# A chain of four blocks: the norm of a block's first batch moved into the tail of the block ahead, and value projections moved to another burst and bank

## The reference, cut to what matters

```python
x = x + tanh(g_xattn[0]) * cross_attention_A(layernorm(x), ctx, mask, bias)   # 16 heads of 16, 512 keys
x = x + tanh(g_ffn[0])   * gated_mixture_B(layernorm(x))                      # 8 heads of 64, causal
x = x + tanh(g_xattn[1]) * cross_attention_C(layernorm(x), ctx)               # 16 heads of 64, 512 keys
x = x + tanh(g_ffn[1])   * product_key_experts_D(layernorm(x))                # top-8 of 64*64 experts
```

```python
q = xn @ w_q; k, v = split(ctx @ w_kv)             # per batch: 512 x 1024 each
attn = softmax(q / 8 @ k.T)                        # per head: 512 x 512
out = (attn @ v) @ w_out + b_out                   # times tanh(gate)
```

## Time and profile before

| | |
|---|---|
| median of three runs | 2357.6 us (2354.5 to 2362.8) |
| the profiled execution: its own time, its span | 2359.9 us, 2358.1 us |
| granted clock of TensorE, mean | 0.974 |
| TensorE busy | 2194.5 us (93%) |
| VectorE busy | 1688.5 us (72%) |
| ScalarE busy | 866.5 us (37%) |
| GpSimd busy | 118.2 us (5%) |
| block A | 0 to 376 us of the span |
| block B | 376 to 1090 us |
| block C | 1090 to 1694 us |
| block D | 1694 to 2358 us |

### The profile page before, as it was taken

The page is one execution under the profiler, slowest core; times in us unless marked ns, Lnnn a source line. Parts: engine busy times, 40 slices in busy tenths (PEclk is TensorE's granted clock), DMA queues, the critical chain, the costliest instruction groups (busy, mean ns, idle before and its releaser), DMA issues. The chain is left out here.

```text
span 2358.1 us, 45622 instructions
## 1 busy us (share of the span) xinstructions
PE 2194.5 (93%) x18214; PEld 1476.8 (63%) x18244; DVE 1688.5 (72%) x4536; ACT 866.5 (37%) x2003; POOL 118.2 (5%) x128
## 2 busy tenths in 40 slices
PE   7999986979999999998899999999779999999998
PEld 3555543444664755775445545555568898989897
DVE  6788873757557556544777777767578888989895
ACT  5787871150330321311555555545321112121110
POOL 3542201000000000000000000000000000000000
PEclk9899987999999999999999999999999999999999
DMA  5011103000000002001000000000200000000000
GB/s 169 22 40 42 27 9 147 0 1 0 1 1 1 1 1 107 1 1 47 1 1 1 1 1 1 1 1 1 107 37 1 2 2 11 2 10 2 1 11 10
DMA packets 23730, 48.62 MB, mean 21 GB/s; under 512 B 4960, under 2 KB 13408, under 8 KB 22880
## 3 DMA queue, kind: packets, MB, share of 16 engines
q1 hardware_dynamic: 23520, 45.71, 5.7%
HBM read 37.57 MB, written 2.10 MB: 17 GB/s over the span
## 5 line engine op out<-in xcount | busy, mean ns | idle before, releaser
L2022 PE MATMUL banks<-work,big 128*128 128x128 f32 x2048 | 251.4, 277 | 0.2 <-issue 0.2
L2022 PEld LDWEIGHTS banks<-work,big 128*128 128x128 f32 x2048 | 245.2, 192 | 4.7 <-issue 0.3
L928 PE MATMUL banks<-big,work 128*128 128x256 f32 x1024 | 241.2, 379 | 3.6 <-issue 3.3
L2133 ACT ACTIVATE work<-banks 128x512 f32<-128x512 f32 x128 | 76.5, 598 | 411.4 <-PE banks L2022 406.7
L854 PE MATMUL banks<-big,work 128*128 128x512 f32 x512 | 221.2, 593 | 0.0
L539 ACT ACTIVATE work<-banks,work 128x512 f32<-128x512 f32 x256 | 174.1, 686 | 121.9 <-DVE work L628 121.8
L928 PEld LDWEIGHTS banks<-big,work 128*128 128x128 f32 x1024 | 195.0, 190 | 33.9 <-issue 1.9
L1689 ACT ACTIVATE work<-work 128x512 f32<-128x512 f32 x256 | 181.0, 711 | 0.0
L854 PEld LDWEIGHTS banks<-big,work 128*128 128x128 f32 x512 | 96.8, 190 | 119.8 <-issue 119.6
L628 DVE TENSOR_REDUCE work<-banks 128x2 f32<-128x1024 f32 x128 | 150.5, 1217 | 14.9 <-PE banks L430 14.9
L1132 DVE CUSTOM_DVE_ANT_0 work<-banks,work 128x512 f32<-128x512 f32 (+3 forms) x128 | 57.7, 488 | 133.2 <-PE banks L870 132.7
(11 more groups left out here) (219 smaller groups left out, 3826.9 us busy)
## 6 DMA issues: line engine op xcount, KB each, us to landing
big<-in_bias SPq DMA_DIRECT2D x16, 256.0 KB, 4.6
big<-in_B_val SPq DMA_DIRECT2D x8, 512.0 KB, 6.9
big<-in_B_out SPq DMA_DIRECT2D x1, 4096.0 KB, 18.7
big<-in_D_downT SPq DMA_DIRECT2D x1, 4096.0 KB, 12.8
big<-in_D_up SPq DMA_DIRECT2D x1, 4096.0 KB, 22.1
work<-work SPq DMA_DIRECT2D x120, 32.0 KB, 2.0
big<-big SPq DMA_DIRECT2D x64, 32.0 KB, 2.0
wc<-in_ctxT SPq DMA_DIRECT2D x1, 2048.0 KB, 7.9
```

The source lines that it names most:

```text
L928: last = eng.matmul(XO[qt // 2][:, qt % 2 * D:(qt % 2 + 1) * D], spread[:, c % NG, qt * P:(qt + 1) * P], w_out[:, c, :], start=False, stop ...
L2022: last = eng.matmul(HP[n % 2][:, q * P:(q + 1) * P], down[:, kc * ELO + n * NJ + q, :], xnT[par][:, kc, :], start=(kc == 0), stop=(kc == K ...
```

## The change

Three edits in one. The norm of batch 0 of B is done in the last steps of A (one part at the end of each of the steps LAST - 3 to LAST + 2), and the norm of batch 0 of C in the steps 4 to 11 of B's last batch; for this `Norm` objects and their semaphores are made before the blocks, in a region of their own, and `xstage` lies at the same place in all three blocks. In B the wait for the constants moves from the head of each engine's stream to the first use: VectorE ahead of `pick_experts(0)`, ScalarE in `take_hits`, TensorE in `choose` (`CONSTS` is 5 + A.groups as before). In C a value projection is issued at u = 0, behind the keys of the next pair, into FB[1], and ScalarE takes it after the two exponentials of tile n; the first four, of batch 0, are issued in the first two bursts instead of before them. The waits on banks follow.

```diff
@@ -139,6 +139,13 @@
         m["s"] = s
+
+        m["stats"] = sb("stats", [P, 128])
+        small, stage = carve(m, "stats"), carve(m)(QT, D)
+        for name, heads, second in (("B", B_, None), ("C", C_, EPS)):
+            turned = Signal(nc, ctx, name + "_xn_transposed", KC)
+            m[name + ".turned"] = turned
+            m[name + ".norm"] = Norm(nc, ctx, m, name, small, second, QT, stage, (turned, KC))
         a_attention(nc, a, m)
@@ -335,7 +342,7 @@
         bo_loaded = ctx.enter_context(nc.semaphore("C_bo_loaded"))
-        xt_made, xt_ready = sig("xn_transposed", KC), sig("xnT_ready", KC)
+        xt_made, xt_ready = m["C.turned"], sig("xnT_ready", KC)
         k_made, k_ready, q_made, q_ready = sig("k_made", T), sig("k_ready", T), sig("q_made", T), sig("q_ready", T)
@@ -344,7 +351,7 @@
         out_made, y_ready, turn_done = sig("out_made", QT), sig("y_ready", QT), sig("x_updated", QT)
-        norm = Norm(nc, ctx, m, "C", take, EPS, QT, xstage, (xt_made, KC))
+        norm = m["C.norm"]
         NORM = [(1, 0), (1, 1), (2, 0), (2, 1), (3, 0), (3, 1), (4, 0), (4, 1)]
@@ -383,9 +390,9 @@
                     elif b == 0 and t == 1:
+                        eng.wait_ge(k_ready.sem, k_ready.at(0, 1))
+                    elif b == 0 and t == 2:
                         eng.wait_ge(v_ready.sem, v_ready.at(0, QT))
-                    elif b == 0 and t == 2:
-                        eng.wait_ge(k_ready.sem, k_ready.at(0, 2))
                     else:
@@ -397,13 +404,19 @@
                     if b == 0 and t == 1:
-                        eng.wait_ge(v_ready.sem, v_ready.at(0, QT))
-                    elif b or t:
+                        eng.wait_ge(v_ready.sem, v_ready.at(0, 1))
+                    elif t == 0 and b:
+                        eng.wait_ge(v_ready.sem, v_ready.at(b, QT - 1))
+                    elif t == 1:
+                        eng.wait_ge(v_ready.sem, v_ready.at(b, QT))
+                    elif 2 <= t <= 5:
+                        eng.wait_ge(v_ready.sem, v_ready.at(b, QT + t - 1))
+                    elif t >= 6 and b < B - 1:
+                        eng.wait_ge(v_ready.sem, v_ready.at(b + 1, t - 5))
+                    elif t >= 6:
                         eng.wait_ge(q_ready.sem, q_ready.at(b, t))
-                        if b > 0 and 3 <= t <= 6:
-                            eng.wait_ge(y_ready.sem, y_ready.at(b - 1, t - 2))
-                        if b < B - 1 and t == T - 1:
-                            eng.wait_ge(xt_ready.sem, xt_ready.at(b + 1, 1))
+                        if t == 6:
+                            eng.wait_ge(y_ready.sem, y_ready.at(b - 1, QT))
                     for kc in range(KC):
@@ -473,32 +486,39 @@
                 queries(0, 0)
-                for kt in range(QT):
-                    if kt >= 2:
-                        eng.wait_ge(v_ready.sem, v_ready.at(0, kt - 1))
-                    elif kt == 0:
-                        eng.wait_ge(k_ready.sem, k_ready.at(0, 1))
-                    else:
-                        eng.wait_ge(q_ready.sem, q_ready.at(0, 1))
-                    values(0, 0, kt, FB[kt % 2])
                 for b, t, u, n in bursts():
+                    if n == 2:
+                        eng.wait_ge(k_ready.sem, k_ready.at(0, 2))
+                        values(0, 0, 1, FB[0])
+                        eng.wait_ge(q_ready.sem, q_ready.at(0, 2))
+                        values(0, 0, 2, FB[1])
                     if n >= 2:
...
                         scores(b, t, u, n, i)
+                    if n == 0:
+                        values(0, 0, 0, FB[1])
+                    if n == 2:
+                        eng.wait_ge(v_ready.sem, v_ready.at(0, 2))
+                        values(0, 0, 3, FB[0])
                     after = (b, t + 1) if t < T - 1 else (b + 1, 0)
...
                         keys(*after)
+                    if u == 0 and n > 2:
+                        if b and 2 <= t <= 5:
+                            eng.wait_ge(y_ready.sem, y_ready.at(b - 1, t - 1))
+                        if b < B - 1 and t >= 6:
+                            eng.wait_ge(xt_ready.sem, xt_ready.at(b + 1, t - 5))
+                        if t == 0:
+                            values(b, 0, QT - 1, FB[1])
+                        elif t <= 4:
+                            values(b, 1, t - 1, FB[1])
+                        elif b < B - 1:
+                            values(b + 1, 0, t - 5, FB[1])
                     if u == 1:
...
                             eng.wait_ge(k_ready.sem, k_ready.at(*after) + 1)
-                        if 1 <= t <= 4:
-                            values(b, 1, t - 1, FB[0])
-                        elif t >= 5 and b < B - 1:
-                            values(b + 1, 0, t - 5, FB[0])
-                        elif t == 0 and b > 0:
-                            values(b, 0, QT - 1, FB[0])
                         if b > 0 and 1 <= t <= 4:
@@ -509,9 +529,7 @@
                     if u == 1 and (b or t):
-                        if b < B - 1 or t <= 4:
-                            eng.wait_ge(v_ready.sem, v_ready.at(b, t + QT))
-                        elif t == T - 1:
+                        if b == B - 1 and t == T - 1:
                             eng.wait_ge(on_ready.sem, on_ready.at(b, T - 2))
@@ -566,25 +584,28 @@
-                norm.all_parts(eng, 0, norm.on_scalar)
-                for kt in range(QT):
-                    take_values(0, 0, kt, FB[kt % 2])
-
                 for b, t, u, n in bursts():
...
                         norm.on_scalar(eng, b + 1, NORM.index((t, u)))
+                    if n == 2:
+                        take_values(0, 0, 1, FB[0])
+                        take_values(0, 0, 2, FB[1])
                     if n >= 2:
...
                     spread_probs(n, 1)
+                    if n == 0:
+                        take_values(0, 0, 0, FB[1])
+                    if n == 2:
+                        take_values(0, 0, 3, FB[0])
+                    if u == 0 and n > 2:
+                        if t == 0:
+                            take_values(b, 0, QT - 1, FB[1])
+                        elif t <= 4:
+                            take_values(b, 1, t - 1, FB[1])
+                        elif b < B - 1:
+                            take_values(b + 1, 0, t - 5, FB[1])
                     spread_probs(n + 1, 0)
-                    if u == 1:
-                        if 1 <= t <= 4:
-                            take_values(b, 1, t - 1, FB[0])
-                        elif t >= 5 and b < B - 1:
-                            take_values(b + 1, 0, t - 5, FB[0])
-                        elif t == 0 and b > 0:
-                            take_values(b, 0, QT - 1, FB[0])
                     if n >= 2:
@@ -658,7 +679,6 @@
                 eng.wait_ge(s["x_loaded"], 16)
-                norm.all_parts(eng, 0, norm.on_vector)
                 for c in range(KC):
@@ -713,9 +733,9 @@
     vtok = wide(QT, A.width)
+    xstage, xnT = take(QT, D), take(KC, S)
     onT = [wide(T, S), take(T, S)]
     pickers = spare(GE, P // 2).bitcast(BF16)
-    xstage, xnT = take(QT, D), take(KC, S)
     qT, kT = take(2, S), spare(2, S)
@@ -734,7 +754,7 @@
         consts = ctx.enter_context(nc.semaphore("B_consts_made"))
-        xt_made, xt_ready = sig("xn_transposed", KC), sig("xnT_ready", KC)
+        xt_made, xt_ready = m["B.turned"], sig("xnT_ready", KC)
         gate_made, gate_ready, pick = sig("gate_made", 1), sig("gate_ready", 1), sig("pick_step", 6)
@@ -745,7 +765,8 @@
         turn_done = sig("x_updated", QT)
-        norm = Norm(nc, ctx, m, "B", take, None, QT, xstage, (xt_made, KC))
+        norm, following = m["B.norm"], m["C.norm"]
+        CONSTS = 5 + A.groups
@@ -911,6 +932,8 @@
                         eng.wait_ge(hit_ready.sem, hit_ready.at(b, 1))
+                        if b == 0:
+                            eng.wait_ge(consts, CONSTS)
                     if b or c:
@@ -930,7 +953,6 @@
                 eng.wait_ge(s["wb_loaded"], 48)
-                eng.wait_ge(consts, 5 + A.groups)
                 for c in range(KC):
@@ -1010,6 +1032,8 @@
                     eng.wait_ge(hit_turned.sem, hit_turned.at(b, 1))
+                    if b < 2:
+                        eng.wait_ge(consts, CONSTS)
                     if b >= 2:
@@ -1052,6 +1074,8 @@
                             norm.on_scalar(eng, b + 1, t * QT + i - 2)
+                        if b == B - 1 and 0 <= t * QT + i - 4 < following.parts:
+                            following.on_scalar(eng, 0, t * QT + i - 4)
                         if len(done) >= 2:
@@ -1183,6 +1206,10 @@
                             norm.on_vector(eng, b + 1, t * QT + i - 2)
+                        if b == B - 1 and 0 <= t * QT + i - 4 < following.parts:
+                            if t * QT + i == 4:
+                                eng.wait_ge(turn_done.sem, turn_done.at(0, QT))
```

(13 more changed lines are left out.)

## The result

The changed kernel takes **2323.7 us** (median of four runs, 2319.7 to 2327.0) where the kernel before takes 2359.0 in the runs beside it (2354.5 to 2362.8): a ratio of 0.985, 95% interval 0.9825 to 0.9875. Forecast was 2320, range 2312 to 2333. The profiled execution has a span of 2323.6 us and a time of its own of 2325.4; mean granted clock 0.977 for 0.974, TensorE busy 2191.2 us, VectorE 1687.2, ScalarE 868.8. The work is the same; of the 34.5 us by which the span is shorter, 31.2 are TensorE's idle time and 3.3 its busy time, which the clock makes longer or shorter.

What follows compares the result with a forecast made beforehand. TensorE's own work bounds the second stage's last batches; its waits at seams and in the third stage can be won. Gains 11.2 + 2.3 + 7.0 + 7.0 + 10.8 = 38.3 us off 2357.6 gave 2319.3, stated 2320, range 2312 to 2333.

Steps and rivals of the forecast that it cites:

- First seam: First to second stage: TensorE starts at 377.2 for 388.48, tail 1.2 us later included; 11.2 us gained.
- The clock term: Second stage's first chain, to the value projections: shorter if the clock stays high; 2.3 us gained, bounds 0 and 4.8.
- Second seam: Second to third stage: TensorE starts at 1090.3 for 1097.28, last batch no longer; 7.0 us gained.
- Start of C: Third stage's start: first scores 15.4 us earlier, less 7.0 for values and 1.4 more; net 7.0 us gained.
- The walk: Third stage, first scores to end of first weighing: 34.7 us, 1.4 more than before; bounds 31.3 and 38.
- The pairs: Third stage's head pairs, values moved to the first burst: 10.8 us gained in sum, bounds 0 and 20.
- Plain pairs: Third stage, six pairs with values but no output projection: 15.77 us, 0.92 less each, 5.5 in all.
- Pairs in which x is turned: Third stage, six pairs turning x in the second burst: 0.1 us less each, 0.6 in all.
- Pairs with a projection: Third stage, pairs with output projection: values' copy already covered; only small waits ahead of transposes won, 1.8 us with ends.
- The weighing's wait: Rival, third stage's pairs: ScalarE's queue brings the wait back, the 10.8 us are gone; 2334 us, chance 0.16.
- Clock held at the seams: Rival, seams and third stage's batch 0: clock stays high, 2.5, 1.7 and 2 us more gained; 2314, chance 0.17.
- The slower case: Rival, 28 pairs: ScalarE's wait for values delays exponentials, some 2 us of lateness per copy; at more 2376, chance 0.03.

Runs made afterwards that it cites:

- e4: Changed kernel with the waits for GpSimd's constants back at the head of the second stage on TensorE and ScalarE: 2331.4 us, ratio 0.9892.
- e5: Changed kernel with ScalarE's norm parts in the first stage's tail one step later, square root behind the last copy: 2320.4 us, ratio 0.9835.
- e2: Kernel before with only the norm of the third stage's batch 0 moved into the second stage's last batch: 2351.1 us, ratio 0.9961.
- e3: Kernel before with only the third stage's value projections moved to the first burst: 2341.7 us, ratio 0.9929.
- e1: Kernel before with only the first seam's edit, norm done ahead and constants awaited at first use: 2347.0 us, ratio 0.9953.
- e8: Changed kernel plus three unused ScalarE copies behind the copy of the values in each of 28 pairs: 2344.6 us, ratio 0.9946.
- e10: Changed kernel run again, unedited: 2319.6 us, ratio 0.9829.
- e9: e5 plus four unused matmuls on TensorE ahead of the first stage's last output projection: 2314.9 us, ratio 0.9813.
- e11: e9 plus four unused 128-column matmuls behind each short step of the second stage's first chain: 2314.2 us, ratio 0.9800.
- e6: Changed kernel with values still in the first burst but in their old bank, FB[0]: 2321.2 us, ratio 0.9839.
- e7: Changed kernel plus one unused ScalarE copy behind the copy of the values in each of 28 pairs: 2325.0 us, ratio 0.9863.
- e12: e9 run again, unedited: 2313.4 us, ratio 0.9805.

## Why the prediction was right

**First seam, 11.2 gained: right.** The idle time fell by 12.4 and the tail's wait rose by 2.40 - 1.21 = 1.2. e4 shows that the two edits share the gain evenly, e5 that the 1.2 are the table load's place. The weights and constants were covered as reckoned: the first value projection starts without a wait, and VectorE waits 6.58 us for constants and then 7.20 for TensorE. What had no term was A's own clock: A ended 6 us later than before in one profile and 1.5 in the next, of which 1.2 are the tail's. The medians' distances from 2320, 3.7 and -0.4, are no larger than that scatter.

**The clock term, 2.3 gained: too large.** With the 13.4 us of idleness ahead the chain took 14.1, 15.8 and 15.8 us (before, e2, e3), mean 15.2; with 1.0 us ahead and no fillers 13.4 to 15.1 in seven profiles (after, e1, e5 to e8, e10), mean 14.2. That is 1.0 where 2.3 stood. The middle of two bounds was a guess, and it weighed three causes: the idle stretch ahead, the wait for the moves before it, and the short waits in between. The first two are not what decides: e9 takes most of the wait for the moves away and the chain stays at 14.9. The third is: e11 fills the small waits inside the chain and it falls to 9.9, which is 5.0 less for the 4.8 of the bound. The Trainium skill (TensorE: Matmul & The Clock Gate, What's actually happening) says that the throttled state is the default and that activity releases it. The trace of e11 agrees: with more activity in the chain, of no use to anyone, none of it was at the lower level.

**Second seam, 7.0 gained: right**, 9.12 - 2.27 = 6.85. B's last batch paid next to nothing: from the first value projection to the last expert 684.7 us for 685.6, and less half of the time at the lower level 680.8 for 680.5.

**Start of C, 7.0 gained: right in sum, and both parts a little off.** Transposes to scores 7.3 us with 3.4 at the lower level, and 6.2 where none of it was (e4, e5, e6, e8), as forecast. The walk took 33.55 us for the 34.7 reckoned: the waits that I put at 1.2 and 1.0 are there (1.24 and 0.96), the first of them for ScalarE's copy of probabilities (L567) where I had named VectorE's; the 1.1 of small ends is not. Together 40.9 for 47.9. In e3, with the 9.1 us of idleness still ahead, the stretch to the scores was 8.7 with 6.3 at the lower level; so 1.4 to 2.5 us here belong to the seam. Most of the 7.0 is clock: 13.1 us at the lower level before and 3.4 after are 4.9 us of it. The forecast had this in its rows, 3.2 us of it by name.

**The pairs, 10.8 gained: right, with its shares spread otherwise.** At equal clock the rest of C fell by 545.5 - 534.5 = 11.0. Plain pairs: 15.65 for the forecast 15.77, so six give 6.2 for 5.5, because the queries don't wait at all. Pairs in which x is turned: 16.37 for 16.69, 0.32 each for 0.1, 1.9 for 0.6; here VectorE's copy leaves 0.27 us of wait. The three of batch 0 took 49.8 us together for 53.1 (54.8, less 1.7 for 3.4 us at the lower level), 3.3 for 2.9. Pairs with a projection gave nothing for the 1.8: they went from 18.92, 19.36, 19.36 and 18.92 to 19.10 each, and in the last batch from 18.92 each to 19.10. The small waits that I counted as won there only changed their place. The sum, 6.2 + 1.9 + 3.3 - 0.4 = 11.0, is right by errors of both signs of up to 2 us, and that is luck.

**The sum.** Behind A's end the profiled executions take 1983.0 us before and 1942.5 after (1942.4 in e10). Less the 1.2 of the tail that is 39.4 gained for the 38.3 forecast. Part of this closeness is luck too: the clock term was 1.7 too large (2.3 for the 0.6 of this pair of profiles), and 1.7 us that no term had came from less time at the lower level in the rest of C.

**The rivals.** The weighing's wait did not come back; e6 shows 4.2 us between copy and weighing even in the old bank. Clock held at the seams: half true, the steps of C from the first scores to the first weighing ran at full clock, the chain in B didn't. The slower case needed ScalarE some 2 us late in each pair, with 1.4 us of cost; e7 and e8 bear out the kind of threshold and give 0.8 to 0.9 us of slack for the 0.6 assumed, with another carrier than the exponentials.

**Best version.** e9 (two medians, 2314.9 and 2313.4) stands 5 to 10 us below the changed kernel's two medians and 43 to 48 us below the kernel before; its ratio to the latter is 0.9813 and 0.9805. Its margin over the changed kernel rests on 1.2 us of tail and some 2 us of output projection, both seen in the traces. The rest is not shown to be the edit's: A had 37.5 and 30.7 us at the lower level in e9 and e12 for 64.9 and 54.6 in the changed kernel's profiles, and 6 to 20 us of that difference lie ahead of the fillers.

## What to carry to other kernels

Idle time of the engine that does the most work, at a change of stage, is found in one row, and the work that ends it can often be done in the stage ahead in gaps of other engines; ask then who waits next (here a table load in ScalarE's queue, and constants that GpSimd makes). If a copy ends a wait right ahead of its use, half a loop's distance can be worth more than another buffer (here the old bank in the new burst kept all of the gain but 2.6 us). Cut the span at the same instructions in both profiles and note the clock level of each stretch, before a difference is put down to an edit: a stage with the same code moved by 6 us.

## What the runs showed of the hardware

- In B's first chain, where TensorE's short matmuls alternate with waits of 0.5 to 0.8 us, 9.1 us or more were at 1.2 GHz in every one of 13 profiles, with 13.4 us of idleness ahead or with 1.0. With the waits filled by matmuls of no use, in one profile, it stayed at 2.4 GHz and the chain went from 14.9 to 9.9 us.
- A wait of 4.7 us for moves by DMA left the projection behind it at 5.3 to 6.8 us; with four matmuls of no use in it, 3.7 us three times out of three.
- Two executions of one kernel had 65 and 55 us at the lower level in a stage of 380 us, and ended it 4.5 us apart; the kernel before, e2 and e3, with one code in it, ended it at 375.1, 377.5 and 381.5.
- A ScalarE table load took 1.28 us, and in a queue without cover cost TensorE 1.2 us (a wait of 2.40 for 1.20).
